# x of channel groups two to four turned by VectorE in 32 by 32 squares, from a new load layout, with SP's waits for it moved

## The chip, the cores and the metric

The kernel runs on one core of one Trainium2 chip. The metric is the device time of one execution in microseconds (us), as the median of several executions. One further execution was recorded by the profiler, and all rows below come from that one.

## The reference, cut to what matters

```python
# x (128, 32, 512), cond_128 (128, 128), fside_S_0 (32,) is the bias
out = lax.conv_general_dilated(x, weight, window_strides=(1,), padding=[(4, 4)],
        dimension_numbers=('NCH', 'OIH', 'NCH'), feature_group_count=4)      # 9 taps, 8 channels in and out per group
h = out + einsum('nd,od->no', c, c_weight)[:, :, None] + bias[None, :, None]
xt = h.reshape(-1, 512)                                                      # 4096 rows
y = (silu(xt @ W_gate.T) * (xt @ W_up.T)) @ W_down.T                         # 512 -> 1376 -> 512
return x + y.reshape(x.shape)
```

## The kernel before, in words

The 32 channels fall into four convolution groups of 8, and the whole kernel goes group by group (`g` = 0 to 3 in the code; "group one" in this text is `g` = 0). A group has 8 channels of 128 samples, so 1024 rows for the feed-forward part, kept as two halves of 512 tokens.

All products are made in fp32r with three terms (hi by hi, lo by hi, hi by lo): ScalarE rounds an operand to its `hi` part and VectorE subtracts it to get the `lo` part. For each of the 11 slices of 128 hidden features (`f`) a first phase makes seven products (`product(g, f, kind)`, kinds 0 to 6) of 6 matmuls each. One pass over such a slice is called an iteration here. ScalarE and VectorE make sigmoid, silu and the gated result from them. A second phase (`down`) multiplies the gated slices with W_down, in 22 units of 12 matmuls.

The convolution of group `g + 1` is woven into the iterations of group `g`. It runs in 8 steps `k` (`k = f - lag(g)`; lag is 1 for `g` = 0, and 0 otherwise). A step covers 64 positions. It needs x with (position, channel) on the partitions and the sample along the row:

- SP loads a chunk of 128 positions (two steps) of x into `x_in` (L344), 512 KB with one DMA. The sample is on the partitions.
- GpSimd copies half of it into `x_blk` with the channel innermost (`block_x`, L305).
- TensorE transposes `x_blk` in four 128 by 128 squares into the bank `xt_ps` (`turn_x`, L604), behind product 1 of the iteration.
- ScalarE makes `xt_hi` from the bank and VectorE `xt_lo` (`split_x`, L843 and L1070).
- TensorE multiplies with the Toeplitz operands made from `toep` (`conv_step`, L624 and L629), behind product 3 of the iteration, for step `k - 1`. The second three matmuls (L629) wait for the split of step `k` as well.
- VectorE adds the context and writes the result into `win` (`read_conv`, L1162). There is one `win` for a chunk, so the first `read_conv` of a chunk waits until the chunk before has left it.
- SP moves `win` into `stage` with one 64 KB DMA for each window of 16 positions (`stage_step`, L336, four DMAs a step). It does so for two steps at once, at the end of every second iteration.

TensorE, ScalarE, VectorE and GpSimd each have their order written out by hand. SP has one too: at each iteration of group one it loads W_gate and W_up for three slices later (`load_nat`), stores the seven split weights of the next slice to DRAM (`save_products`, L365), and in later groups it refills the ring of 16 slots from there (`refill`, L389, seven an iteration), each slot when the product that used it is done. At the end of the iteration come the load of x (after `x_blocked`) and the staging.

In group one the weights are also made: TensorE transposes the W_gate and W_up slices (`turn_gate`, `turn_up`), ScalarE and VectorE split them, and GpSimd mixes two of the seven (`mix_t`, `mix_t_lo`). `copy_chain` (L843) carries the sums from one product to the next through ScalarE.

## Time and profile before

| | us |
|---|---|
| median of 3 runs | 764.38 (764.04 to 764.9) |
| the profiled execution | 765.41 |
| its span, first to last instruction | 763.6 |
| mean granted TensorE clock | 0.999 |

The span is what the rows cover; 1.8 us of the profiled execution lie around it. Start times in rows are us from the start of the span. A matmul's record overlaps the next one's, so the pace of TensorE is read from the starts, not from the durations. For two or more merged instructions of a line (x2, x4) the time is that of the merged stretch.

### The profile page before, as it was taken

The numbers are of one execution on the slowest core, as the hardware profiler recorded it, in microseconds if no ns is written. First come the engines' busy times: TensorE is split into PE (matmuls) and PEld (weight loads), VectorE is DVE, ScalarE is ACT, GpSimd is POOL, SyncE is SP. The second block draws the span as 40 slices with busy tenths as digits, with TensorE's granted clock in tenths as the row PEclk, the third lists the DMA queues.
The fourth block names the chain that finished last, engine by engine and source line by source line (L and its number), as shares of the span: only waits on it lengthen the run. The fifth ranks groups of instructions, "written<-read, shape, count | busy, mean of one in ns | idle before, by whom it ended". The sixth has DMA issues, their size and how long they took to land.

```text
span 763.6 us, 10287 instructions
## 1 busy us (share of the span) xinstructions
PE 749.9 (98%) x3465; PEld 611.4 (80%) x3465; DVE 426.9 (56%) x703; ACT 275.3 (36%) x519; POOL 79.6 (10%) x111
## 2 busy tenths in 40 slices
PE   7989999999999999999999999999999999999998
PEld 6768888878888887887888878787788888887886
DVE  3897776764765555446735545445763444445224
ACT  4555555443433233324422332233431233333221
POOL 4334434110000111001000100100000000000000
PEclk9999999999999999999999999999999999999999
DMA  6486666679988578667435867667443876766412
GB/s 184 125 316 235 222 226 236 219 221 312 356 266 262 166 206 221 172 179 218 163 114 187 268 176 209 193 191 218 140 140 109 295 197 195 193 191 181 140 27 111
DMA packets 113684, 152.37 MB, mean 200 GB/s; under 512 B 11138, under 2 KB 49186, under 8 KB 113634
## 3 DMA queue, kind: packets, MB, share of 16 engines
q1 hardware_dynamic: 113152, 151.51, 63.7%
q8 instruction: 29, 0.48, 0.3%
q10 hardware_dynamic: 482, 0.21, 0.1%
q14 instruction: 21, 0.17, 0.1%
HBM read 108.95 MB, written 34.34 MB: 188 GB/s over the span
## 4 chain that ended last, share of the span: by engine, by line
PE 90%; issue 3%; SPq 2%; DMA 2%; DVE 1%; POOL 1%; ACT 0%; POOLq 0%; DVEq 0%
PE bank L711 51%; PE bank L774 31%; PE bank L624 2%; PE bank L629 2%; PE bank L604 2%; SPq L336 2%; DMA stage<-win 1%; PE bank L667 1%; PE bank L638 1%; PE bank L649 0%; DVE g_all L1277 0%; POOL g_all L526 0%; PE bank L586 0%; DVE win L1162 0%; POOL t_all L513 0%
## 5 line engine op out<-in xcount | busy, mean ns | idle before, releaser
L711 PE MATMUL bank<-hc_hi,ring 128*128 128x512 f32 (+1 forms) x1204 | 376.5, 394 | 5.0 <-DVE ring L1070 2.0
L711 PEld LDWEIGHTS bank<-hc_hi,ring 128*128 128x128 f32 (+1 forms) x1204 | 219.5, 185 | 54.6 <-issue 5.0
L711 PE MATMUL bank<-hc_lo,ring 128*128 128x512 f32 (+1 forms) x602 | 235.1, 391 | 0.0
L774 PE MATMUL bank<-ring,g_hi 128*128 128x512 f32 (+1 forms) x704 | 218.6, 392 | 0.0
L774 PEld LDWEIGHTS bank<-ring,g_hi 128*128 128x128 f32 (+1 forms) x704 | 131.2, 188 | 28.0 <-DVE g_lo L1070 0.8
L843 ACT ACTIVATE mix<-bank 128x512 f32<-128x512 f32 (+1 forms) x129 | 77.1, 598 | 208.5 <-PE bank L711 208.5
L774 PE MATMUL bank<-ring,g_lo 128*128 128x512 f32 (+1 forms) x352 | 137.1, 390 | 0.0
L711 PEld LDWEIGHTS bank<-hc_lo,ring 128*128 128x128 f32 (+1 forms) x602 | 111.5, 185 | 26.2
L1070 DVE TENSOR_TENSOR g_lo<-g_all,g_hi 128x512 fp32r<-128x512 f32 (+1 forms) x88 | 60.9, 695 | 83.7 <-ACT g_hi L843 83.7
L843 ACT ACTIVATE g_hi<-g_all 128x512 fp32r<-128x512 f32 (+1 forms) x88 | 55.1, 629 | 114.1 <-PE bank L774 114.0
L1243 DVE TENSOR_TENSOR mix<-bank,mix 128x512 f32<-128x512 f32 (+1 forms) x43 | 29.7, 691 | 87.2 <-ACT mix L960 87.0
L774 PEld LDWEIGHTS bank<-ring,g_lo 128*128 128x128 f32 (+1 forms) x352 | 66.1, 188 | 14.1
L305 POOL COPY x_blk<-x_in 128x512 f32<-128x512 f32 x24 | 28.0, 1166 | 325.5 <-DMA x_in<-in_x 166.4
L1238 DVE TENSOR_TENSOR mix<-bank,mix 128x512 f32<-128x512 f32 (+1 forms) x43 | 29.5, 687 | 37.5 <-ACT mix L843 37.5
L1233 DVE TENSOR_TENSOR mix<-mix 128x512 f32<-128x512 f32 (+1 forms) x43 | 29.7, 692 | 34.8 <-ACT mix L954 34.7
L960 ACT ACTIVATE mix<-bank 128x512 f32<-128x512 f32 (+1 forms) x43 | 25.7, 598 | 43.2 <-PE bank L711 43.2
L1228 DVE TENSOR_TENSOR mix<-bank,mix 128x512 f32<-128x512 f32 (+1 forms) x43 | 29.7, 691 | 11.2 <-PE bank L711 6.0
L843 ACT ACTIVATE xt_hi<-bank 128x512 fp32r<-128x512 f32 (+1 forms) x33 | 15.9, 510 | 55.1 <-PE bank L604 55.1
L1248 DVE TENSOR_TENSOR mix<-bank,mix 128x512 f32<-128x512 f32 (+1 forms) x43 | 29.7, 691 | 8.1 <-PE bank L711 6.8
L1162 DVE TENSOR_TENSOR win<-bank,ctxb 128x512 f32<-128x512 f32 (+1 forms) x24 | 16.1, 670 | 30.4 <-DMA stage<-win 21.5
L1070 DVE TENSOR_TENSOR hc_lo<-stage,hc_hi 128x512 fp32r<-128x512 f32 x50 | 32.6, 691 | 0.8 <-ACT hc_hi L843 0.7
L843 ACT ACTIVATE hc_hi<-stage 128x512 fp32r<-128x512 f32 x50 | 28.6, 618 | 2.9 <-DMA stage<-g_all 2.8
(141 smaller groups left out, 562.1 us busy)
## 6 DMA issues: line engine op xcount, KB each, us to landing
ring<-saved SPq DMA_DIRECT2D x319, 256.0 KB, 2.9
saved<-ring SPq DMA_DIRECT2D x99, 256.0 KB, 2.6
g_all<-in_x SPq DMA_DIRECT2D x32, 256.0 KB, 3.7
out_y<-g_all SPq DMA_DIRECT2D x32, 256.0 KB, 3.6
x_in<-in_x SPq DMA_DIRECT2D x13, 512.0 KB, 5.1
stage<-win SPq DMA_DIRECT2D x96, 64.0 KB, 2.8
w_nat<-in_L_ffn_W_gate SPq DMA_DIRECT2D x10, 256.0 KB, 3.9
w_nat<-in_L_ffn_W_up SPq DMA_DIRECT2D x10, 256.0 KB, 3.9
```

What stands on the lines that cost most here:

```text
L305: copy(blocks(grp, k)[:, :, :, :], x_place(grp, k // 2)[:, :, r0:r0 + WB * R] .rearrange("n c (b r) -> n b r c", r=R)).then_inc(x_blocked_ ...
L711: mm = pe.matmul(bank[0:w, :], wt, hv, start=fresh and q == 0 and t == 0, stop=q == 1 and t == 2, skip_group_check=not fresh)
L774: mm = pe.matmul(acc(half, tt)[:], gs, wd, start=f == 0 and t == 0, stop=f == FC - 1 and t == 2)
L843: return act.activation(dst, src, ACT.Copy)
L960: act.activation(act_b[0:w], chain_ps[f % 2][0:w, :], ACT.Sigmoid).then_inc(sig_b_done, 1)
L1070: return dve.tensor_tensor(dst, src, hi_part.bitcast(F32), ALU.subtract)
L1162: last = dve.tensor_tensor(to[:, w0:w0 + n, :], conv_bank(grp, k)[:, 0:n * P].rearrange("p (w n) -> p w n", w=n), ctxb[:, grp:grp + 1, :]. ...
L1228: dve.tensor_tensor(act_a[0:w], second_ps[0:w, :], copy0[0:w], ALU.add).then_inc(gate_a_done, 1)
L1233: dve.tensor_tensor(act_a[0:w], act_a[0:w], sig_a[0:w], ALU.mult).then_inc(silu_a_done, 1)
L1238: dve.tensor_tensor(copy4[0:w], third_ps[0:w, :], copy4[0:w], ALU.add).then_inc(up_b_done, 1)
L1243: dve.tensor_tensor(act_b[0:w], chain_ps[f % 2][0:w, :], act_b[0:w], ALU.mult).then_inc(silu_b_done, 1)
L1248: dve.tensor_tensor(copy2[0:w], third_ps[0:w, :], copy2[0:w], ALU.add).then_inc(up_a_done, 1)
```

## The change

For groups two to four x no longer goes through GpSimd and TensorE. SP loads each chunk with eight DMAs of 64 KB instead of one of 512 KB: partition `32 quad + n` of `x_in` gets, for both channels of the pair `quad`, the samples `n`, `n + 32`, `n + 64` and `n + 96`. VectorE turns half of such a chunk in one instruction, in squares of 32 by 32, into `x_blk` (now also seen as `x_turn`), with (channel, position) on the partitions. ScalarE and VectorE split that directly from there. VectorE does this at the head of the iteration, ahead of `gate_a`.

The partitions now have the channel outermost and the position in it innermost, so the rows of `toep` for groups two to four are put in that order once: GpSimd makes a permutation matrix `reorder`, TensorE multiplies `toep` with it in three matmuls of 192 columns (behind product 1 of the first iteration, where the first transposes of group two were), and ScalarE copies the results back ahead of its first Toeplitz split. The wait of TensorE for the last residual sums goes from `turn_x` to `conv_head`.

SP's work for the convolution goes to the head of its iteration. Each step is staged alone (four DMAs in every iteration for `k` = 2 to 9, instead of eight in every second one). The loads of chunks 1 to 3 come at `k` = 1, 3, 5 and wait for the turn of step `k`, where they came at the ends of `k` = 0, 2, 4 behind GpSimd's copy.

```diff
@@ -116,6 +116,7 @@
             x_gate = sb("x_gate", [P, KC, P], F32, early)
             t_all = sb("t_all", [P, 4, 2, P], F32, early)
             up1 = sb("up1", [P, TOK], F32R, early)
+            reorder = sb("reorder", [P, P], F32, early)
         g_hi = sb("g_hi", [P, NG, TOK], F32R)
         g_lo = sb("g_lo", [P, NG, TOK], F32R)
         stage = sb("stage", [P, KC, CG, P])
@@ -305,6 +306,15 @@
             copy(blocks(grp, k)[:, :, :, :], x_place(grp, k // 2)[:, :, r0:r0 + WB * R]
                  .rearrange("n c (b r) -> n b r c", r=R)).then_inc(x_blocked_first if grp == 0 and k == 0 else x_blocked, 1)
 
+
+
+        QUAD = 32
+        NB, CQ = P // QUAD, CG // (P // QUAD)
+        x_turn = x_blk[:, :, :, :].rearrange("n b r c -> n (b r c)")
+
+        def x_split_from(grp, k):
+            return xt_bank(grp, k)[:] if grp == 0 else x_turn
+
         def xt_at(grp, k):
             return (k if grp == 0 else k % 2) * WB * P
 
@@ -341,8 +351,15 @@
         @block.sync
         def _(sp):
             def load_x(grp, i):
+                if grp > 0:
+                    for quad in range(NB):
+                        for c in range(CQ):
+                            sp.dma_start(x_in[quad * QUAD:(quad + 1) * QUAD, c::CQ, :],
+                                         x[:, grp * CG + quad * CQ + c, i * P:(i + 1) * P].rearrange("(b n) l -> n b l", b=NB)
+                                         ).then_inc(x_loaded, LD)
+                    return
                 sp.dma_start(x_place(grp, i), x[:, grp * CG:(grp + 1) * CG, i * P:(i + 1) * P]
-                             ).then_inc(x_first_loaded[i] if grp == 0 else x_loaded, LD)
+                             ).then_inc(x_first_loaded[i], LD)
 
             def load_nat(f):
                 w = width(f)
@@ -429,6 +446,15 @@
                 if g > 0:
                     refill(product_at(g, 0, 0))
                 for f in range(FC):
+                    k = f - lag(g)
+                    if g + 1 < G and k == 2:
+                        for kind in range(KINDS):
+                            sp.wait_ge(hc_done[kind], hc_count(g, 1, kind))
+                    if g + 1 < G and 2 <= k < STEPS + 2:
+                        stage_step(g + 1, k - 2)
+                    if g + 1 < G and k in (1, 3, 5):
+                        sp.wait_ge(x_turned, STEPS * (g + 1) + k + 1)
+                        load_x(g + 1, (k + 1) // 2)
                     if g == 0 and f + 3 < FC:
                         load_nat(f + 3)
                     if g == 0 and f == FC - 2:
@@ -438,20 +464,10 @@
                         save_products(f + 1)
                     for fk in phase1[7 * f + 1:7 * f + 8]:
                         refill(product_at(g, *fk))
-                    k = f - lag(g)
-                    if g + 1 < G and k in (0, 2, 4):
-                        sp.wait_ge(x_blocked, STEPS * (g + 1) + k + 1)
-                        load_x(g + 1, k // 2 + 1)
-                    if g + 1 < G and k == 2:
-                        for kind in range(KINDS):
-                            sp.wait_ge(hc_done[kind], hc_count(g, 1, kind))
-                    if g + 1 < G and k in (2, 4, 6, 8):
-                        stage_step(g + 1, k - 2)
-                        stage_step(g + 1, k - 1)
                 if g == 0:
                     save_down(0)
                 if g + 2 < G:
-                    sp.wait_ge(x_blocked, STEPS * (g + 2) - 1)
+                    sp.wait_ge(x_turned, STEPS * (g + 2))
                     load_x(g + 2, 0)
                 for m, (f, half) in enumerate(units(g)):
                     if g == 0 and half == 0 and f + NDOWN < FC:
@@ -486,13 +502,8 @@
                                pattern=[[-1, TAPS], [-TAPS, CG]], channel_multiplier=1).then_inc(consts, 1)
 
             def block_x(grp, k):
-                if grp == 0:
-                    pool.wait_ge(x_first_loaded[k // 2], LD)
-                else:
-                    pool.wait_ge(x_loaded, LD * (KC * (grp - 1) + k // 2 + 1))
-                if grp > 0:
-                    pool.wait_ge(x_turned, STEPS * grp + k)
-                elif k > 1:
+                pool.wait_ge(x_first_loaded[k // 2], LD)
+                if k > 1:
                     pool.wait_ge(x_turned, k - 1)
                 copy_block(pool.tensor_copy, grp, k)
 
@@ -536,6 +547,8 @@
             block_x(0, 5)
             block_x(0, 6)
             block_x(0, 7)
+            pool.wait_ge(consts, 8)
+            pool.tensor_copy(reorder[:].rearrange("p (m r) -> p m r", r=R), ident[:].rearrange("p (r m) -> p m r", r=R)).then_inc(consts, 1)
             wrap(1)
             mix_t(0)
             mix_t_lo(0)
@@ -543,15 +556,11 @@
             mix_h_first(1)
             for g in range(G):
                 for f in range(FC):
-                    if g + 1 < G and f == 0:
-                        block_x(g + 1, 0)
                     if g == 0 and f + 2 < FC:
                         wrap(f + 2)
                     if g == 0 and f + 1 < FC:
                         mix_t(f + 1)
                         mix_t_lo(f + 1)
-                    if g + 1 < G and lag(g) <= f < STEPS - 1 + lag(g):
-                        block_x(g + 1, f + 1 - lag(g))
 
         @block.tensor
         def _(pe):
@@ -588,23 +597,32 @@
                 mm.then_inc(toep_mm, 1)
 
             def turn_x(grp, k):
-                if grp == 0 and k == 0:
+                if k == 0:
                     pe.wait_ge(x_blocked_first, 1)
-                else:
-                    pe.wait_ge(x_blocked, STEPS * grp + k)
-                if grp == 0 and k == 0:
                     pe.wait_ge(conv_w_ready, 1)
-                elif grp == 0 and k > 1:
+                else:
+                    pe.wait_ge(x_blocked, k)
+                if k > 1:
                     pe.wait_ge(xt_lo_done, k - 1)
-                elif grp > 0:
-                    pe.wait_ge(xt_lo_done, STEPS * grp + k)
-                if k == 0 and grp >= 2:
-                    pe.wait_ge(y_added, 2 * OB * (grp - 1))
                 for b in range(WB):
                     mm = pe.transpose(xt_bank(grp, k)[:, b * P:(b + 1) * P], blocks(grp, k)[:, b, :, :], ident[:])
                 mm.then_inc(x_turned, 1)
 
+            def reorder_toep():
+
+                pe.wait_ge(toep_done, 2)
+                pe.wait_ge(consts, 9)
+                pe.wait_ge(xt_lo_done, STEPS)
+                pe.wait_ge(g_done[1], 1)
+                for grp in range(1, G):
+                    to = conv_ps if grp == G - 1 else xt_ps
+                    at = (grp - 1) % 2 * QN * CG
+                    mm = pe.matmul(to[:, at:at + QN * CG], reorder[:], toep[:, grp, :, :], start=True, stop=True)
+                mm.then_inc(toep_mm, 1)
+
             def conv_head(grp):
+                if grp > 1:
+                    pe.wait_ge(y_added, 2 * OB * (grp - 1))
                 pe.wait_ge(t_lo_done, grp + 1)
                 pe.wait_ge(xt_lo_done, STEPS * grp + 1)
                 if grp == 1:
@@ -811,8 +829,8 @@
                         turn_up(2)
                     if conv and k == 1:
                         conv_head(g + 1)
-                    if conv and 0 <= k < STEPS:
-                        turn_x(g + 1, k)
+                    if g == 0 and k == 0:
+                        reorder_toep()
                     if g == 0 and f == FC - 1:
                         turn_down(0)
                     product(g, f, 2)
@@ -847,6 +865,11 @@
                     act.wait_ge(toep_done, 2)
                 else:
                     act.wait_ge(conv_done, CPG * grp)
+                if grp == 1:
+                    act.wait_ge(toep_mm, 2)
+                    hi(toep[:, 1:G - 1, :, :], xt_ps[:, 0:(G - 2) * QN * CG].rearrange("p (g q o) -> p g q o", g=G - 2, o=CG))
+                    hi(toep[:, G - 1, :, :], conv_ps[:, 0:QN * CG].rearrange("p (q o) -> p q o", o=CG)).then_inc(toep_done, 1)
+                    act.wait_ge(toep_done, 3)
                 hi(ta_hi[:], toep[:, grp:grp + 1, HALO:QN, :])
                 hi(tb_hi[:, TB0:P], toep[:, grp:grp + 1, 0:HALO, :]).then_inc(t_hi_done, 1)
 
@@ -855,9 +878,9 @@
                     act.wait_ge(conv_done, CPG * grp + (k if k >= 2 else 0))
                 act.wait_ge(x_turned, STEPS * grp + k + 1)
                 at = xt_at(grp, k)
-                last = hi(xt(grp)[0][:, at:at + WB * P], xt_bank(grp, k)[:])
+                last = hi(xt(grp)[0][:, at:at + WB * P], x_split_from(grp, k))
                 if grp > 0 and k % 2 == 0 and k > 0:
-                    last = hi(xt_hi[:, 2 * WB * P:], xt_bank(grp, k)[:, 0:P])
+                    last = hi(xt_hi[:, 2 * WB * P:], x_turn[:, 0:P])
                 last.then_inc(xt_hi_done, 1)
 
             def take_slot(s):
@@ -1107,12 +1130,21 @@
                     lo(t[0], toep[:, grp, HALO:QN, :], t[1])
                     lo(t[2][:, R - HALO:, :], toep[:, grp, 0:HALO, :], t[3][:, R - HALO:, :]).then_inc(t_lo_done, 1)
 
+            def turn_x(grp, k):
+                dve.wait_ge(x_loaded, LD * CG * (KC * (grp - 1) + k // 2 + 1))
+                if grp == 1 and k == 0:
+                    dve.wait_ge(x_turned, STEPS)
+                else:
+                    dve.wait_ge(xt_lo_done, STEPS * grp + k)
+                l0 = k % 2 * WB * R
+                dve.transpose(x_turn, x_in[:, :, l0:l0 + WB * R].rearrange("p m (w r) -> p w m r", r=R)).then_inc(x_turned, 1)
+
             def split_x(grp, k):
                 dve.wait_ge(xt_hi_done, STEPS * grp + k + 1)
                 at = xt_at(grp, k)
-                last = lo(xt(grp)[1][:, at:at + WB * P], xt_bank(grp, k)[:], xt(grp)[0][:, at:at + WB * P])
+                last = lo(xt(grp)[1][:, at:at + WB * P], x_split_from(grp, k), xt(grp)[0][:, at:at + WB * P])
                 if grp > 0 and k % 2 == 0 and k > 0:
-                    last = lo(xt_lo[:, 2 * WB * P:], xt_bank(grp, k)[:, 0:P], xt_hi[:, 2 * WB * P:])
+                    last = lo(xt_lo[:, 2 * WB * P:], x_turn[:, 0:P], xt_hi[:, 2 * WB * P:])
                 last.then_inc(xt_lo_done, 1)
 
             def w_lo(f, kind, src):
@@ -1318,6 +1350,8 @@
                     n, k = FC * g + f, f - lag(g)
                     more = g == 0 and f + 1 < FC
                     last = f == FC - 1
+                    if conv and 0 <= k < STEPS:
+                        turn_x(g + 1, k)
                     gate_a(n, f)
                     if conv and k == 1:
                         read_head(g + 1)
```

## Rows read from the trace of the kernel before

**Rows 1.** The page: busy time of each engine, and the granted TensorE clock in 40 slices.
```profile
PE 749.9 (98%) x3465; PEld 611.4 (80%) x3465; DVE 426.9 (56%) x703; ACT 275.3 (36%) x519; POOL 79.6 (10%) x111
...
PEclk9999999999999999999999999999999999999999
```

**Rows 2.** The chain that ended last: start, us, what (two pieces).
```profile
302.95 0.44 PE bank L604 x4
...
595.16 102.17 PE bank L711 x450
```

**Rows 3.** Windows, one iteration of group one, one of group two: length, busy times.
```profile
77.84:90.20 12.36, 12.36 (x62) 10.18 (x61) 8.78 (x17) 6.57 (x15) 4.56 (x7) 1.00 0.65 210
247.90:259.29 11.39, 11.39 (x53) 9.39 (x53) 6.18 (x11) 3.68 (x7) 2.23 (x2) 1.00 0.61 172
```

**Rows 4.** Timeline, first iteration (f = 1): start, us, engine, line, what [idle before <-releaser].
```profile
47.38 0.60 PE L604 MATMUL bank<-ident,x_blk 128*128 128x128 f32 x4
49.95 0.73 PE L711 MATMUL bank<-hc_hi,ring 128*128 128x512 f32 x2 [1.97 <-DVE ring L1070]
...
57.35 0.70 PE L711 MATMUL bank<-hc_hi,ring 128*128 128x512 f32 x2 [1.20 <-issue]
...
47.95 0.69 DVE L1221 TENSOR_TENSOR g_all<-bank,mix 128x512 f32<-128x512 f32 x1
48.56 1.33 DVE L1070 TENSOR_TENSOR ring<-t_all,ring 128x256 fp32r<-128x256 f32 x2
...
56.67 0.58 ACT L843 ACTIVATE mix<-bank 128x512 f32<-128x512 f32 x1
```

**Rows 5.** Timeline, setup: matmuls in plain f32 of 128 columns (two records each).
```profile
30.11 0.49 PE L576 MATMUL bank<-g_all 128*128 128x128 f32 x2
...
30.95 0.49 PE L576 MATMUL bank<-g_all 128*128 128x128 f32 x2
```

**Rows 6.** The page, groups of instructions: xcount | busy us, mean ns | idle before, releaser.
```profile
L305 POOL COPY x_blk<-x_in 128x512 f32<-128x512 f32 x24 | 28.0, 1166 | 325.5 <-DMA x_in<-in_x 166.4
...
L1228 DVE TENSOR_TENSOR mix<-bank,mix 128x512 f32<-128x512 f32 (+1 forms) x43 | 29.7, 691 | 11.2 <-PE bank L711 6.0
```

**Rows 7.** Timeline of PE and DVE, iterations f = 4 and 5 of group one.
```profile
85.62 0.62 PE L711 MATMUL bank<-hc_hi,ring 128*128 128x512 f32 x2
...
90.89 0.40 PE L629 MATMUL bank<-xt_hi,tb_hi 128*128 128x512 f32 x1
...
86.43 0.68 DVE L1261 TENSOR_TENSOR g_all<-mix 128x512 f32<-128x512 f32 x1
87.03 0.68 DVE L1257 TENSOR_TENSOR g_all<-mix 128x512 f32<-128x512 f32 x1
...
89.12 0.68 DVE L1070 TENSOR_TENSOR xt_lo<-bank,xt_hi 128x512 fp32r<-128x512 f32 x1
...
101.48 0.88 DVE L1070 TENSOR_TENSOR xt_lo<-bank,xt_hi 128x512 fp32r<-128x512 f32 x2
```

**Rows 8.** Timeline of DVE and PE, iteration f = 2 of group two.
```profile
257.44 0.89 DVE L1070 TENSOR_TENSOR xt_lo<-bank,xt_hi 128x512 fp32r<-128x512 f32 x2
...
259.82 0.40 PE L629 MATMUL bank<-xt_hi,tb_hi 128*128 128x512 f32 x1
```

**Rows 9.** Two lines of SP: ns to issue one DMA (min/median/max), us to landing.
```profile
L336 SPq DMA_DIRECT2D stage<-win x96: 552/598/1657, 85.0 to 522.0; - x96
...
DMA to landing us min/median/max: 2.4/2.6/4.5
...
L344 SPq DMA_DIRECT2D x_in<-in_x x13: 379/426/943, 1.2 to 472.2; - x13
```

**Rows 10.** Timeline of SP, end of iteration f = 4 of group two.
```profile
290.07 5.08 SPq L336 DMA_DIRECT2D stage<-win  x8
```

**Rows 11.** Who waited for whom: us in total, times, longest us.
```profile
DVE win L1162 <- DMA stage<-win: 21.5, 6, 4.4
...
PE bank L711 <- DVE mix L1238: 1.9, 3, 0.8
```

More of the change, by code:

```diff
@@ L590, in turn_x @@
             def turn_x(grp, k):
-                if grp == 0 and k == 0:
+                if k == 0:
                     pe.wait_ge(x_blocked_first, 1)
+                    pe.wait_ge(conv_w_ready, 1)
                 else:
-                    pe.wait_ge(x_blocked, STEPS * grp + k)
-                if grp == 0 and k == 0:
-                    pe.wait_ge(conv_w_ready, 1)
-                elif grp == 0 and k > 1:
+                    pe.wait_ge(x_blocked, k)
+                if k > 1:
                     pe.wait_ge(xt_lo_done, k - 1)
-                elif grp > 0:
-                    pe.wait_ge(xt_lo_done, STEPS * grp + k)
-                if k == 0 and grp >= 2:
-                    pe.wait_ge(y_added, 2 * OB * (grp - 1))
                 for b in range(WB):
```

## The prediction, made before the changed kernel was run

> **What bounds the kernel now.** I read the page first. TensorE is busy for 749.9 of 763.6 us at a granted clock that never leaves its upper level (2.4 GHz), VectorE for 56%, GpSimd for 10% [rows 1]. So the question is only what TensorE issues and where it waits. The chain that ended last gives its pace: 450 matmuls of 512 columns in 102.17 us, 0.227 us each, and four transposes of x take 0.44 us of it [rows 2]. The windows then show the two kinds of iteration. One of group one is 12.36 us long and one of group two 11.39, TensorE is busy in all of both, VectorE in 8.78 and 6.18 [rows 3]. Where x is turned, TensorE is therefore the bound, with other engines close only in group one. The waits say where it stands still after the first iteration: 1.9 us in three places, behind `up_b` (L1238), which stands on VectorE behind a `read_conv` that waited for the staging DMAs for up to 4.4 us [rows 11]. The timeline of the first iteration shows two more stops, of 1.97 and 1.20 us, where VectorE's and ScalarE's backlog from the setup sets the time [rows 4].
>
> **What is removed.** TensorE loses 24 blocks of four transposes (three groups, eight steps). Each is on the path, so 24 x 0.44 = 10.56 us go [rows 2]. One block is an exception: the first, at 47.38, stands ahead of the stop that ends at 49.95 [rows 4], so its 0.44 us was time in which TensorE would have waited anyway. That leaves 10.12. GpSimd's 24 copies (28.0 us, [rows 6]) were beside everything, so they are worth nothing by themselves.
>
> **What VectorE gets.** 24 turns of 128x512. The trace has no such operation. From below it is bounded by nothing I can defend except a small part of a normal instruction, so I take 0.30 us. From above by GpSimd's copy of the same half chunk in 16-element runs, 1.17 us. The nearest row is a VectorE pass over 128x512 f32, which lasts 0.69 us and costs 0.60 when another follows at once (86.43 to 87.03) [rows 6, 7]. I take 0.60, since the turn, too, reads and writes each element once.
>
> The Trainium skill (VectorE: DVE Perf Modes, The three transpose paths) gives 311 ns for a turn of 128x128 in bf16 on VectorE. As an estimate from that page, four such widths would be 1.24 us if time grew with width, and the sum would come out near the dear case below. No row here shows it.
>
> The turn stands ahead of `gate_a` and `split_x`, so each `xt_lo` ends 0.60 later against the end of the iteration before, while TensorE asks for it 0.44 earlier. It asks at the first L629. In group one, iteration f = 4, `xt_lo` ends at 89.80 and L629 starts at 90.89: margin 1.09, after the change 1.09 - 0.44 - 0.60 = 0.05. For even k it is 102.36 against 90.89 + 12.36 = 103.25: 0.89 - 1.04 = -0.15 [rows 3, 7]. Three such steps (k = 2, 4, 6) cost 0.45. In group two the margin at an even k is 259.82 - 258.33 = 1.49, so 0.45 stays [rows 8], and there the turn is free. Without that margin it would cost up to 0.60 in each of 16 iterations. What waits behind the turn on VectorE (`gate_a`, the weight splits, silu) is used by TensorE later than this.
>
> **The first iteration.** VectorE works without a gap from about 44 to 57 us there, and the stop that ends at 57.35 is for `copy_chain` of kind 4, which ScalarE ends at 57.25 behind `t_all` from VectorE [rows 4]. The first turn goes straight into this backlog: +0.60. The three matmuls of `reorder_toep` stand where the first transposes were, and wait for the first gated result of the second half, at 48.64. Plain f32 matmuls of 128 columns come in pairs 0.84 apart, 0.42 each [rows 5], so one of 192 columns is at most 0.63 and three 1.9. They end near 50.5 instead of 49.95; TensorE then reaches the second stop 0.6 later, at 56.75, and still has to wait until 57.95. So they cost nothing beyond the 0.60, and 1.9 if the stops were not there. ScalarE's two copies of `toep` out of the banks are each no longer than the 0.58 of a 128x512 one [rows 4], and `copied2` is ready about when TensorE asks for it, 2.7 us after 50.5. GpSimd's one copy into `reorder` lies in setup ahead of a wait for VectorE; it is at most a full 128x512 copy, 1.17.
>
> **What SP gets.** A load of a chunk becomes eight DMAs of 64 KB. The nearest row is the staging DMA of the same size: 0.60 to issue (at most 1.66) and 2.6 to land (at most 4.5); a whole chunk took 0.43 to issue [rows 9]. So a load is 4.8 us instead of 0.4, for 12 loads some 52 us more of SP. SP now also waits at the head of iterations k = 1, 3, 5, for a turn that ends at 87.63 + 0.60 = 88.23, which is 2.6 us after the iteration's start [rows 7]. Behind this wait stand the eight loads, then `load_nat`, `save_products` and the refills. The refills have 16 slots of six matmuls as lead, 16 x 1.36 = 21.8 us, against a delay of about 7.4 (2.6 + 4.8), and a landing of a few us. The saved weights and next slices of W are used more than an iteration later. So this is hidden. For x itself: issued at 7.4, landed by 10.0 to 11.9, and wanted by VectorE 11.39 - 0.44 + 2.0 = 12.95 after the same start. One to three us are left.
>
> The Trainium skill (DMA: Bandwidth & Descriptors, Measured) speaks against this edit: it advises batching to 1 MiB and calls transfers under 64 KB dominated by descriptors. In the trace eight pieces of 64 KB are issued in 5.08 us and overlap in flight [rows 9, 10], so the rule bears on SP's time and not on when x is there.
>
> **What the staging gives.** Before, SP issued two steps together in 5.08 us, from 290.07 on [rows 10], behind seven refills and the load of x; `read_conv` waited for the last. Now the first half has gone an iteration earlier and the second is first in SP's queue: issued by 2.4 after the head, landed by 5.0 to 6.9, about when `read_conv` wants to run. VectorE's six waits (21.5 us) should shrink to at most 1 or 2 us each, and TensorE's 1.9 us with them [rows 11]. I take 1.85 as gain; if it doesn't come, nothing.
>
> **Sum.** -10.12 + 0.60 + 0.45 - 1.85 = -10.92. Against the profiled execution that is 765.41 - 10.92 = 754.5. The median shown is 1.03 lower, so 753.5.
>
> **Rivals.**
> - *The turn is dear* (1.17). For: x is read in runs of 16, and GpSimd's copy was slow. Against: each element still passes once. The first iteration costs 0.57 more; group one's margins become -0.52 (four odd steps) and -0.72 (three even), 4.24 in place of 0.45; later even steps lose 0.12 six times. 753.5 + 0.57 + 3.79 + 0.7 = 758.5.
> - *Group one doesn't get shorter.* VectorE has 9.4 of 11.9 us to do there in a fixed order, and its chain through ScalarE may simply become the pace. Then its seven 0.44 are not gained: 753.5 + 3.1 - 0.45 = 756.1. Against: TensorE has no wait there now.
> - *The staging gain stays out*: 755.4.
> - *x comes too late, and the kernel is slower.* One mechanism: SP's issue of a piece. If it takes d us and lands in 2.6, VectorE stands at the head of the next iteration from 2.6 + 8d + 2.6 > 13.4 on, so d > 1.02, and all of TensorE's inputs behind it. Nine loads (k = 1, 3, 5 in three groups) are exposed. The whole gain is eaten at 1.2 us each, d = 1.17; at d = 1.3 nine times 2.2 us give 773. For: a DMA with four runs a partition may be slower than any shown, and the largest staging issue is 1.66. Against: the medians.
> - *The change does nothing for the time*, because TensorE's freed slots turn into waits everywhere: 764.4. Nothing in [rows 3] speaks for it, as TensorE never pauses there.
>
> By the figure of the Trainium skill above the dear case would be the likeliest; no row of VectorE shows it.
>
> **Chances.** My sum 0.68 (own range 752.4 to 754.6), the dear turn 0.10, group one at its old length 0.08, no staging gain 0.06, x too late 0.06, nothing 0.02. A measurement of this kernel tells 0.2% (1.5 us) from no change. Faster: 0.92, within: 0.02, slower: 0.06. The range: down to 751.5 (a turn of 0.30 takes 0.3 and the 0.45 off, and the chain of the first iteration may fall to GpSimd's lighter load), up to the dear turn, 758.5.
>
> **What would show it.** After the change: no L604 after the first 30 us, three f32 matmuls near 49 us; the iteration of group one at 11.9 to 12.1 us and of group two at 10.95; VectorE's turn at 0.6 to 0.7; each x piece issued in about 0.6 us; no wait of `win` for the stage DMAs of over 2 us; the stop near 58 us still there. The prediction is wrong if the turn takes over 1.2 us, if VectorE shows long waits for `x_in`, or if TensorE shows waits for `xt_lo` in most iterations.

## The result

| | us |
|---|---|
| before, median of 4 runs | 764.64 (764.04 to 767.55) |
| changed, median of 4 runs | 753.26 (751.9 to 754.21) |
| ratio | 0.9854, 95% interval 0.9834 to 0.9873 |
| span of the profiled execution, before and after | 763.6 and 750.7 |

The changed kernel is 11.4 us faster by the medians, and 12.9 by the two profiled executions. The forecast was 753.5, with a range of 751.5 to 758.5. (The median before is higher than in the table ahead of the prediction because a fourth run, of 767.55, has been added.)

The page after the change, busy times, against [rows 1]:

```profile
PE 738.9 (98%) x3375; PEld 602.0 (80%) x3375; DVE 437.6 (58%) x727; ACT 274.6 (37%) x521; POOL 51.4 (7%) x88
```

TensorE has 90 matmuls fewer (96 transposes gone, three f32 matmuls of two records each come) and 11.0 us less of busy time, and it is as full as before. VectorE got 10.7 us more. Three windows after the change, two iterations of group one (odd k, even k) and one of group two, against [rows 3]:

```profile
89.16:101.06 11.90, 11.90 (x57) 9.74 (x56) 9.21 (x18) 6.48 (x16) 3.55 (x6) 1.00 0.78 258
101.06:113.16 12.10, 12.10 (x58) 9.71 (x56) 9.42 (x19) 6.69 (x16) 3.49 (x6) 1.00 0.65 226
244.34:255.27 10.93, 10.93 (x49) 9.01 (x48) 6.26 (x10) 3.07 (x8) 0.00 (x0) 1.00 0.75 229
```

A block of four transposes was worth 0.46 us: 12.36 to 11.90, and 11.39 to 10.93. In group one every even k gives 0.2 of it back.

The turn on VectorE and the pieces of x on SP, one line each (ns min/median/max), against [rows 6, 9]:

```profile
L1140 DVE STREAM_TRANSPOSE x_blk<-x_in x24: 700/704/708, 49.2 to 484.5; 128x512 f32<-128x512 f32 x24
...
L357 SPq DMA_DIRECT2D x_in<-in_x x96: 311/432/1294, 35.8 to 467.8; - x96
...
DMA to landing us min/median/max: 1.8/2.1/5.3
```

The turn took 0.70 us, about as a plain VectorE pass over 128x512 f32 (0.69), and not the 1.24 us estimated from the Trainium skill's bf16 figure (VectorE: DVE Perf Modes, The three transpose paths); a piece took 0.43 us to issue and not 0.60.

Waits after the change, against [rows 11]:

```profile
DVE win L1194 <- PE bank L647: 8.6, 16, 0.9
...
PE bank L729 <- issue: 1.4, 1, 1.4
```

No `read_conv` waits for the staging any more. Of TensorE's five stops of over 0.3 us from the first iteration to the last convolution step, two in the first iteration and three behind `up_b`, the two of the first iteration are left. The second of them ends where it did (57.35 before, [rows 4]):

```profile
48.77 1.21 PE L620 MATMUL bank<-toep,reorder 128*128 128x192 f32 x6 [1.93 <-DVE g_all L1253]
...
57.34 0.70 PE L729 MATMUL bank<-hc_hi,ring 128*128 128x512 f32 x2 [1.42 <-issue]
```

The account, from the starts of the 24 convolution steps in both traces: the first step comes 0.40 us earlier, the eighth and last in group one's iterations 2.50, the first in those of group two 3.40, the last there 7.43, the first in those of group three 8.32, the last there 12.85, and the rest of the span is as long as before. Inside groups two and three, iterations without a stop went from 11.4 to 10.93. The four with a stop had been 11.63, 12.37, 12.47 and 12.02 long, that is 0.21, 0.95, 1.05 and 0.60 above 11.4, and are 10.93 too: the stops were worth 2.8 us with the slower matmuls behind them. 23 blocks at 0.46 are 10.6. With the 2.8, and less 0.6 for the even k, this is 12.8.

### The profile page after: what moved, and what is told of

The parts are those of the page before. It is cut to its first block, busy times and chain, and to the rows that moved or that the text cites. A ratio compares the mean times of both kernels' runs of the same rounds, so it can differ in the third digit from the quotient of the medians.

```text
span 750.7 us, 10175 instructions
## 1 busy us (share of the span) xinstructions
PE 738.9 (98%) x3375; PEld 602.0 (80%) x3375; DVE 437.6 (58%) x727; ACT 274.6 (37%) x521; POOL 51.4 (7%) x88
## 4 chain that ended last, share of the span: by engine, by line
PE 94%; DVE 2%; DMA 1%; SPq 1%; ACT 1%; issue 1%; DVEq 0%
PE bank L729 55%; PE bank L792 32%; PE bank L647 3%; PE bank L642 3%; DVE hc_lo L1093 1%; SPq L346 1%; PE bank L685 1%; DMA x_in<-in_x 1%; PE bank L656 1%; PE bank L608 0%; PE bank L667 0%; DMA stage<-g_all 0%; DVE g_all L1309 0%; DVE g_all L1194 0%; DVE ring L1093 0%
## 5 line engine op out<-in xcount | busy, mean ns | idle before, releaser
L983 ACT ACTIVATE mix<-bank 128x512 f32<-128x512 f32 (+1 forms) x43 | 25.7, 598 | 43.2 <-PE bank L729 43.2
L861 ACT ACTIVATE xt_hi<-x_blk 128x512 fp32r<-128x512 f32 (+1 forms) x33 | 16.9, 539 | 65.2 <-DVE x_blk L1140 65.2
L1289 DVE TENSOR_TENSOR g_all<-mix 128x512 f32<-128x512 f32 (+1 forms) x43 | 29.4, 685 | 0.0
L1293 DVE TENSOR_TENSOR g_all<-mix 128x512 f32<-128x512 f32 (+1 forms) x43 | 29.3, 682 | 0.0
```

Source lines behind the costliest of these rows:

```text
L861: return act.activation(dst, src, ACT.Copy)
L983: act.activation(act_b[0:w], chain_ps[f % 2][0:w, :], ACT.Sigmoid).then_inc(sig_b_done, 1)
L1289: dve.tensor_tensor(g_all[0:w, f, 0, :], copy2[0:w], act_a[0:w], ALU.mult).then_inc(g_done[0], 1)
L1293: dve.tensor_tensor(g_all[0:w, f, 1, :], copy4[0:w], act_b[0:w], ALU.mult).then_inc(g_done[1], 1)
```

## The experiments

### The staging alone, in the kernel before

```diff
                 for f in range(FC):
+                    k = f - lag(g)
+                    if g + 1 < G and k == 2: (waits for hc_done)
+                    if g + 1 < G and 2 <= k < STEPS + 2:
+                        stage_step(g + 1, k - 2)
...
-                    if g + 1 < G and k in (2, 4, 6, 8):
-                        stage_step(g + 1, k - 2)
-                        stage_step(g + 1, k - 1)
```

> The kernel before with one edit of the change alone: SP stages each step by itself at the head of its iteration, the loads of x stay where they were. Theory: TensorE's four stops behind the staging in groups two and three go (their iterations of 11.63, 12.37, 12.47 and 12.02 us become 11.4), so 2.8 us less, 761.8 against 764.6, and no iteration of group one changes. Rival (the whole gain is that of TensorE's freed slots and the staging gives nothing): 764.6.

Measured: 762.48 us (10 runs) against 764.75, ratio 0.9969 (0.9955 to 0.9983). All iterations of groups two and three are 11.39 to 11.42 long, and VectorE's wait is

```profile
DVE win L1161 <- DMA stage<-win: 8.2, 4, 2.6
```

So this edit of SP alone is worth 2.3 us by the medians (1.3 to 3.4 by the interval), and it needs nothing of the rest.

### The old staging, in the changed kernel

The same edit backwards in the changed kernel: staging in pairs, at the end of every second iteration, all else as changed.

> The changed kernel with SP's staging put back in pairs at the end of every second iteration; all else as changed. Theory: VectorE's long waits for the staging come back in groups two and three, 21 us in six places, and TensorE stops in four of them for 0.2 to 1.2 us, a little longer than before since its iteration is 0.46 shorter: 2.8 to 4 us more, 756 to 757.3 against 753.3. Rival (in the new kernel VectorE and SP have room enough, since the load of x is no longer ahead of the staging there): under 1 us more.

Measured: 753.08 us, ratio to before 0.9845 (0.9824 to 0.9866), no different from the changed kernel. VectorE did wait:

```profile
DVE win L1195 <- DMA stage<-win: 14.9, 6, 3.0
```

but no wait was over 3.0 us, and TensorE never stopped. The theory failed: pairs at the end of an iteration are not what stopped TensorE. What the two kernels with pairs differ in on SP is the load of x, which the changed kernel no longer has ahead of them.

### The load of x behind the staging, in the kernel before

```diff
-                    if g + 1 < G and k in (0, 2, 4): (wait, load_x)
                     if g + 1 < G and k == 2: ...
                     if g + 1 < G and k in (2, 4, 6, 8):
                         stage_step(g + 1, k - 2)
                         stage_step(g + 1, k - 1)
+                    if g + 1 < G and k in (0, 2, 4): (wait, load_x)
```

> The kernel before, with only the order at the end of SP's iteration turned round: the pairs of staging first, then the load of x, still one DMA of 512 KB. Theory now: what made TensorE stop was the load issued right ahead of the staging; its 512 KB stand in the DMA queue before the windows, and the last window lands 3.9 us after its issue instead of about 2. With the load behind, read_conv waits under 3 us and TensorE's four stops go: 2.5 us less, 762.2, as when the staging was moved to the head. Rival (the stops come from the pairs being issued late, at the end of the iteration): 764.7.

Measured: 762.64 us (10 runs), ratio 0.9974 (0.9965 to 0.9983). No iteration of groups two and three has a stop. The waits are those of the run before:

```profile
DVE win L1162 <- DMA stage<-win: 14.9, 6, 3.0
...
DMA to landing us min/median/max: 2.3/2.6/3.6
```

Against [rows 11] the longest wait is 1.4 us shorter, and against [rows 9] the longest landing is 3.6 and not 4.5. At the same place of group two (284 to 300 us) the median landing of the eight windows was, before,

```profile
stage<-win SPq DMA_DIRECT2D x8, 64.0 KB, 3.8
```

and with the load behind

```profile
stage<-win SPq DMA_DIRECT2D x8, 64.0 KB, 2.8
```

The six places with a pair of staging show the cause. In the kernel before, four of them stand behind a load of x, and the median landings there are 3.1, 3.8, 3.7 and 3.7 us; the two without a load have 2.8 and 2.5. With the load behind, all six have 2.5 to 2.8. From the end of the last window's issue to `read_conv` it was 1.85, 3.35, 3.26 and 2.78 us behind a load, and it is 1.8 to 1.9 in all other cases of both traces. So at three places the windows landed later behind the 512 KB; at the first only SP's own time for the load (0.94 there) came ahead of them.

How late `read_conv` may be can be read from the kernel before, too. Its six waits were 3.51, 4.25, 3.23, 4.38, 3.90 and 2.28 us, three of them here:

```profile
274.72 0.69 DVE L1162 TENSOR_TENSOR win<-bank,ctxb 128x512 f32<-128x512 f32 x1 [3.51 <-DMA stage<-win]
...
321.28 0.69 DVE L1162 TENSOR_TENSOR win<-bank,ctxb 128x512 f32<-128x512 f32 x1 [3.23 <-DMA stage<-win]
...
457.08 0.69 DVE L1162 TENSOR_TENSOR win<-bank,ctxb 128x512 f32<-128x512 f32 x1 [4.38 <-DMA stage<-win]
```

The iterations with 3.51, 4.25, 4.38 and 3.90 are the four long ones, by 0.21, 0.95, 1.05 and 0.60 us, which is each time the wait less 3.3; those with 3.23 and 2.28 are not longer. A wait of `read_conv` costs TensorE nothing up to 3.3 us in this kernel, and all of what is above. Either of the two edits of SP's order keeps every wait under that, so the second has no stop left to remove (the two together were not run in the kernel before).

### Eight pieces, in the kernel before

```diff
             def load_x(grp, i):
+                if grp > 0:
+                    for c in range(CG):
+                        sp.dma_start(x_in[:, c, :], x[:, grp * CG + c, i * P:(i + 1) * P]).then_inc(x_loaded, LD)
+                    return
```

GpSimd's wait for the load counts all eight pieces.

> The kernel before, with each load of x of groups two to four made as eight DMAs of 64 KB, one for each channel, into the old layout. Theory: SP spends some 0.43 us on each piece, 3 us more for a load; the loads stand ahead of the staging at the ends of k = 2 and 4 there, so read_conv waits some 3 us longer in those four places of groups two and three, and TensorE with it: 764.6 + 4 x 2.5 to 3 = 775. In group one nothing. Rival (pieces are free wherever they stand): 764.6.

Measured: 784.02 us, ratio 1.0241 (1.0216 to 1.0266): slower than the theory said, by 9 us. Four iterations took 15.71, 17.71, 15.87 and 15.66 us instead of 11.4, and two of group one 13.4 and 13.2. One of the stops, and the granted clock behind it (last but two column of the windows):

```profile
280.58 1.19 PE L715 MATMUL bank<-hc_hi,ring 128*128 128x512 f32 x2 [2.71 <-DVE mix L1242]
```

```profile
276.00:280.00 4.00, 1.88 (x9) 1.22 (x7) 0.85 (x2) 1.20 (x2) 0.00 (x0) 1.00 0.61 168
280.00:282.00 2.00, 1.42 (x4) 1.16 (x4) 1.03 (x2) 0.00 (x0) 0.00 (x0) 0.51 0.94 282
282.00:284.00 2.00, 2.00 (x7) 1.62 (x6) 0.48 (x1) 0.00 (x0) 0.00 (x0) 0.63 0.74 280
284.00:286.00 2.00, 2.00 (x12) 1.66 (x12) 1.87 (x4) 0.55 (x2) 0.51 (x1) 1.00 0.68 161
```

The stop itself is 2.71 us, and the iteration is 4.3 us longer, because TensorE was then granted 1.2 GHz for about 3 us. Behind the longest stop, of 3.28 us, the granted clock was 0.50 from 308 to 314 us, and that iteration is the 17.71. In group one the theory had seen no cost, and there were stops of 0.79 and 0.59. Eight pieces at the old place in SP's order are a loss of 19 us. (These pieces are one channel each over 128 partitions, and not the 32 partitions by four runs of the changed kernel; a piece of either kind is 64 KB.)

### TensorE's slots put back

```diff
+                    if conv and 0 <= k < STEPS and g + k > 0:
+                        ... (waits for the bank)
+                        for b in range(WB):
+                            pe.transpose(xt_ps[:, b * P:(b + 1) * P], ident[:], ident[:])
```

> The changed kernel with 23 blocks of four transposes of the identity matrix put back where the transposes of x were (all but the first block); their result is used by nobody. Theory: TensorE's slots alone are worth 23 x 0.46 = 10.6 us, less 0.6 since the three overshoots of xt_lo in group one vanish: 763.3. Rival (the freed slots gave less, and the gain is from GpSimd's and ScalarE's relief): under 5 us more.

Measured: 764.07 us (10 runs), 10.8 above the changed kernel. Iterations are 12.36, 11.39 and 11.42, those of the kernel before without its stops. From the first convolution step to the last it is 9.54 us longer than the changed kernel: 22 blocks lie between those steps, and 22 x 0.46 less 0.6 is 9.5. The rest lies ahead of the first step: one more block, and the first iteration, where the granted clock of this profiled execution fell for a few us (0.83 and 0.74 in the stretches 48 to 52 and 52 to 56). So the freed slots carry about 10 us, and the relief of GpSimd in the iterations after the first nothing.

### Each turn twice

```diff
+                dve.transpose(x_turn, x_in[...]).then_inc(turned_once, 1)
+                dve.wait_ge(turned_once, STEPS * (grp - 1) + k + 1)
                 dve.transpose(x_turn, x_in[...]).then_inc(x_turned, 1)
```

> The changed kernel with each turn made twice on VectorE, the second after the first by a semaphore, 0.7 us more at the head of 24 iterations. Theory: the turn is at the edge of its cover. The trace of the changed kernel has xt_lo ready 0.2 us ahead of its first user at even k in group two and 0.1 us late in group one, so most iterations with a turn get 0.3 to 0.7 us longer: 8 to 12 us more in all, 761 to 765. Rival (VectorE has 42% idle, a turn more is hidden): under 2 us more.

Measured: 766.7 us (10 runs), ratio to before 1.0021 (1.0005 to 1.0037): 13.4 above the changed kernel, a little over the theory's range, and the whole gain is gone. TensorE waits for it directly:

```profile
PE bank L648 <- DVE xt_lo L1094: 7.3, 13, 0.7
```

Iterations are 12.6 to 12.86 in group one and 11.13 to 11.71 in two and three. From the first convolution step to the last it is 12.25 us longer than the changed kernel: 0.7 for each turn of k = 1 to 7 in group one, and 0.2 to 0.4 for the odd and 0.8 for the even steps in groups two and three. The turns of k = 0 in groups two and three cost nothing, since VectorE waits there anyway. (The rest of the 13.4 lies ahead of the first step, where the first turn stands. There, too, the granted clock of the profiled execution fell, 0.78 and 0.79 in the stretches 56 to 60 and 60 to 64.) So 0.7 us on an engine that is idle for 42% of the span costs on average nearly 0.6 in each of 21 iterations: the idle time lies elsewhere in the iteration. In the changed kernel's iteration f = 2 of group two the margin is 0.21 us: `xt_lo` ends at 255.75 and L647 starts at 255.96.

```profile
253.20 0.71 DVE L1140 STREAM_TRANSPOSE x_blk<-x_in 128x512 f32<-128x512 f32 x1
254.86 0.89 DVE L1093 TENSOR_TENSOR xt_lo<-x_blk,xt_hi 128x512 fp32r<-128x512 f32 x2 [0.38 <-ACT xt_hi L861]
...
255.96 0.41 PE L647 MATMUL bank<-xt_hi,tb_hi 128*128 128x512 f32 x1
```

### Sixteen pieces

Each load of x cut once more, two blocks of samples a piece, 32 KB each.

> The changed kernel with each load of x cut once more, sixteen DMAs of 32 KB. Theory: a piece costs SP 0.43 us, so a load takes 7 us instead of 3.7; the last piece lands by 2.6 + 7 + 2.1 = 11.7 us after the head of the iteration, VectorE wants it at 12.9: no change, 753.3. Rival (SP is already at its limit): VectorE waits for x_in at even k, and the time rises by 5 us or more.

Measured: 755.98 us, ratio 0.9884 (0.9854 to 0.9914), 2.7 above the changed kernel: between the two. In groups two and three the theory held but for one iteration of 11.1. In group one, where SP has the weights to move as well, VectorE waited for x once, TensorE with it, and TensorE for the slices of W_down twice:

```profile
DVE x_blk L1141 <- DMA x_in<-in_x: 1.1, 1, 1.1
PE bank L686 <- DMA w_nat<-in_L_ffn_W_down: 0.7, 2, 0.4
```

```profile
128.21 0.47 PE L648 MATMUL bank<-xt_hi,tb_hi 128*128 128x512 f32 x1 [1.12 <-DVE xt_lo L1094]
```

The iteration with that stop was the longest of group one, 13.24 us, and the way from group one's last step to the first of group two was 1.1 us longer, of which 0.7 are the two waits for W_down. A load did not take SP 7 us but 8.4 to 8.8 in group one, against 3.7 to 3.9 in the changed kernel. So the rival with x too late has its mechanism right, and it starts near the 8.2 us for a load (8 x 1.02) that the prediction gave: the loads of 7.6 to 8.1 us in group two cost nothing. Of the time lost, 2.6 us lie between the first convolution step and the last.

### GpSimd's copies put back

A copy of 128x512 into a spare tile at each old place in group one.

> The changed kernel with GpSimd's eight copies of 128x512 put back at their old places of group one; they copy the context sums into a spare tile that nobody reads. Theory: in the first iteration the turn's 0.6 us was paid for by GpSimd being through with its mixing earlier, so that VectorE's two splits of t_all took 0.75 and not 1.33 us; with the copy back the stop of TensorE that ends at 57.34 ends 0.5 to 0.7 us later, and the time is 0.6 us more, 753.9; the iterations after it stay as they are. Rival (the compensation came from somewhere else): the stop ends at 57.3 as before.

Measured: 753.81 us, ratio 0.9849 (0.9819 to 0.9879), and the stop ended at 57.06. But the first copy had no x to wait for and ran long before its old place, so this run tells nothing about the first iteration. It does show that the other seven copies cost nothing. The next run has one copy, behind the wait:

```diff
+            pool.wait_ge(x_loaded, LD * CG)
             for g in range(G):
                 for f in range(FC):
+                    if g == 0 and f == 0:
+                        pool.tensor_copy(spare, ctxb in 16-element runs)
```

> The changed kernel with one copy of 128x512 on GpSimd ahead of the first mixing of the loop, and this time behind a wait for the first chunk of group two, as in the kernel before. Theory: in the kernel before, GpSimd waited for that chunk until 43.3 us and then copied, and VectorE's splits of 48.6 us ran beside its mixing (1.33 us for the two); without both, VectorE got 0.58 us back, which paid the first turn. With both back the two splits take 1.3 us again and the stop of TensorE near 57.3 ends 0.5 us later. Rival (it is not GpSimd): 0.75 us for the splits, the stop ends where it did.

Measured: a single run, 753.24 us, so there is no interval. The first iteration, against [rows 4]:

```profile
43.49 1.11 POOL L559 COPY spare<-ctxb 128x512 f32<-128x512 f32 x1 [14.46 <-DMA x_in<-in_x]
...
48.05 1.41 POOL L533 TENSOR_TENSOR ring<-t_all,ring 128x256 fp32r<-128x256 f32 x2
```

```profile
48.75 1.33 DVE L1101 TENSOR_TENSOR ring<-t_all,ring 128x256 fp32r<-128x256 f32 x2
```

```profile
58.13 0.70 PE L737 MATMUL bank<-hc_hi,ring 128*128 128x512 f32 x2 [1.78 <-issue]
```

In the changed kernel the same two splits of VectorE were

```profile
43.64 3.66 DVE L1093 TENSOR_TENSOR hc_lo<-g_all,hc_hi 128x512 fp32r<-128x512 f32 x4
...
48.54 0.75 DVE L1093 TENSOR_TENSOR ring<-t_all,ring 128x256 fp32r<-128x256 f32 x2
```

because GpSimd's mixing was over by 46.15. With the copy back they take 1.33 us and the stop ends 0.79 later. Of the 0.79 only 0.56 is the copy's: VectorE is 0.23 us behind already at 42.54, against 42.31 in the changed kernel, before the copy starts, and so its four `hc_lo` splits begin at 43.87 and not at 43.64. The Trainium skill (SBUF — State Buffer, SBUF: two separate sides) says that a VectorE instruction with two SBUF inputs and a GpSimd instruction that reads SBUF hold one pair of ports in turn; the two lengths agree with it.

A trace with the real copy shows that these 0.58 us need not be lost there. In the kernel before with the staging moved, x came earlier, GpSimd copied at 41.08, and its mixing fell on the four `hc_lo` splits:

```profile
43.20 4.10 DVE L1069 TENSOR_TENSOR hc_lo<-g_all,hc_hi 128x512 fp32r<-128x512 f32 x4
...
48.55 0.75 DVE L1069 TENSOR_TENSOR ring<-t_all,ring 128x256 fp32r<-128x256 f32 x2
```

So the sum counts. From the start of the `hc_lo` splits to the pass that follows the two splits, or the turn behind them, it was 5.94 us before; 6.02, 6.28 and 5.57 in the three other traces of that kernel with another order or size of loads; 5.57 in the changed kernel without the turn's 0.63; and 6.13 here without it. With the copy VectorE loses 0 to 0.7 us more to GpSimd in the first iteration than without it, depending on what the mixing falls on, and 0.37 in the pair compared.

### The turn in VectorE's gap

```diff
-                    if conv and 0 <= k < STEPS:
-                        turn_x(g + 1, k)
+                    if conv and k == 0:
+                        turn_x(g + 1, 0)
                     gate_a(n, f)
...
                     up_b(n, f)
+                    if conv and 0 <= k < STEPS - 1:
+                        turn_x(g + 1, k + 1)
```

> The changed kernel with the turns of steps 1 to 7 moved from the head of their iteration into the one before, between up_b and silu_b, where VectorE waits 1.9 us for ScalarE's sigmoid. Theory: the 0.2 us that each even k of group one lost come back (iterations of 12.1 become 11.9), nothing else moves: 0.6 us less, 752.7. Rival (a turn there meets x_in before it has landed, since SP loads it in the same iteration): TensorE waits at odd k, 1 to 3 us more in nine places.

Measured: 752.92 us, ratio to before 0.9841 (0.9812 to 0.9871). From the first convolution step to the last it is 431.52 us long and the changed kernel 432.37, and group one's iterations are 11.87 to 11.91. VectorE waited three times for x, 1.6 us in all, at no cost. By the medians 0.3 us is less than the runs can tell. Its profiled execution shows one reason why it isn't more. After the first stop in the first iteration the granted clock fell:

```profile
44.00:48.00 4.00, 3.37 (x19) 2.58 (x17) 4.00 (x6) 2.44 (x6) 2.68 (x3) 1.00 0.96 331
48.00:52.00 4.00, 2.69 (x8) 2.63 (x9) 3.96 (x9) 0.44 (x2) 0.37 (x2) 0.68 1.02 378
52.00:56.00 4.00, 4.00 (x17) 3.23 (x17) 3.21 (x8) 3.68 (x10) 0.00 (x0) 0.90 1.00 324
```

```profile
49.30 2.16 PE L620 MATMUL bank<-toep,reorder 128*128 128x192 f32 x6 [1.94 <-DVE g_all L1253]
```

The three reorder matmuls took 2.16 us there and 1.21 in the trace of the changed kernel.

### The gap, and the stop filled

```diff
                 pe.wait_ge(xt_lo_done, STEPS)
+                for b in range(4 * WB):
+                    pe.transpose(xt_ps[:, b % WB * P:(b % WB + 1) * P], ident[:], ident[:])
                 pe.wait_ge(g_done[1], 1)
```

> The kernel with the turn in VectorE's gap, and sixteen transposes of the identity ahead of the three reorder matmuls, where TensorE otherwise stands still for 1.9 us; nobody uses their result. Theory: in some executions (mean clock 0.998) the granted clock fell to 1.2 GHz for a few us right after this stop, which cost 1.5 to 2 us; with the stop filled the clock stays at 2.4 GHz in all, and the median is that of the undisturbed ones with the turn in the gap, about 751.8. Rival (the fall of the clock has nothing to do with the stop, or the transposes make TensorE late): 752.9 or more, and runs at 0.998 as before.

Measured: 752.09 us (751.8 to 753.03, 4 runs), ratio to before 0.9837 (0.9824 to 0.9851). The mean clock was 0.999 or 1.000 in all four; of the four runs of the changed kernel two were at 0.998, and these took 754.0 and 754.2 against 751.9 and 752.5. The five runs with the turn in the gap alone were at 0.997 to 0.999. It is the fastest kernel of the study by its median, but its interval overlaps that of the changed kernel, so it is not shown to be faster than that one, only than the kernel before. Four runs do not settle either that the stop was the cause of the fall.

## Why the prediction was right

**What bounds the kernel** held. TensorE was full before and is full after, and about 10 us came with its slots, as the run with idle transposes shows.

**The price of a block** was 0.44 in the sum and 0.46 in the windows, probably since the first matmuls behind a block are a little slower and the piece of the chain didn't hold that. Over 23 blocks that is 0.5 us.

**The first block as an exception** held: both stops of the first iteration are still there, and the first convolution step came 0.40 us earlier, one block's worth and not two.

**The first iteration** (+0.60) was wrong, the measured value is -0.01. VectorE's turn did go into its backlog, and cost 0.63. Two things that the sum left out hid it. GpSimd's copy, costed at nothing, had held back its mixing, and without the copy VectorE lost 0.37 us less to GpSimd. And VectorE's row of passes began 0.23 earlier in the trace after (43.64 against 43.87). That is scatter: over all traces, of either kernel, it begins between 43.2 and 45.0. So the term by itself was 0.26, and that the stop ended at the same time is chance.

**The turn's 0.60** held (0.70 long, it costs 0.62 to 0.63 ahead of another pass). The margins were less sound than they looked. For even k of group one a loss of 0.15 was forecast and 0.2 measured. For group two 0.45 was forecast and 0.21 measured, since `xt_lo` now waits for ScalarE's `xt_hi`, which starts only after the turn. It was enough, and the double turn shows how little more was there.

**SP's load**: 3.7 to 3.9 us instead of 4.8 (the first one 4.5), landed in time. This step held, and the sixteen pieces show the point from which it no longer does. One slip stands in the rival on x: it lets VectorE ask for x at 13.4, where the working above it has 12.95. With 12.95 its limit is 0.97 us for a piece and not 1.02.

**The staging** (-1.85) had the sign right, the size too small (2.8 by the trace, 2.3 and 1.8 by the medians of the two runs in the kernel before) and the reason half right. I took the stops' waiting time, and the slower matmuls behind each and the fourth, short stop of 0.21 were not in it. As the reason I named the place of the pairs, behind seven refills and the load of x. The runs show that the load ahead is enough of a cause: with the pairs at their old place behind the refills and the load put behind them, all stops are gone, as they are with the staging moved to the head.

The larger errors in size all go one way and add up: 0.6 too much cost in the first iteration, and some 1.0 and 0.5 too little gain in staging and slots. Only the even k go the other way, with 0.15 too little cost. Together this takes the forecast gain from 10.9 to 12.9, that of the profiled pair. So the mechanism was right, but that the median lies within 0.3 us of the forecast is in part luck. The forecast was counted down from the profiled execution of the kernel before (765.41) and then lowered by its distance to the median. The median of four runs before is 764.64, 0.8 under that execution, and the median after is 0.7 above its own profiled one. Two of the four runs after, at a mean clock of 0.998, took some 2 us more than the others; where in them the clock fell is not recorded. Why the medians before lie below the profiled execution no run shows, only that the staging is worth 2.3 and 1.8 us by medians and 2.8 by that trace.

Of the rivals, the dear turn is ruled out by its 0.70 us, group one at its old length by the windows. That x comes too late was not the case but near, and the case without a staging gain is ruled out by the trace.

## What to carry to other kernels

Work moved off a full engine is worth its slot there, but price it at the place where it lands: an engine with 42% idle had 0.2 us free at the point that mattered. A large load issued right ahead of small transfers that somebody waits for can cost them more than its issue (here 0.4 us of issue, and 1.0 to 1.5 us of landing at three places of four); order SP's work by who waits, and cut or place loads behind. And price the removed work of an idle engine too: by what stood behind it, and by whom it slowed.

## What was not expected of the hardware

- Each of the four stops of TensorE of 2.4 to 3.3 us in groups two and three of the run with eight pieces was followed by 1.2 GHz, for some 3 us behind three of them and for over 6 us behind the longest, so that a stop of 2.71 us made an iteration 4.3 us longer. In the first iteration the length of the stop did not decide it. Stops of 1.92 to 1.94 us were followed by a fall in the traces of the sixteen pieces, the idle transposes and the turn in the gap. The stops of 1.93 and 1.97 us in the changed kernel and the kernel before were not, and neither was one of 2.77 us in the run with eight pieces. What decides it stays open.
- A pass of VectorE in 32 by 32 squares over 128x512 f32, read in 16-element runs, took 0.70 us, the same as a plain one.
- Two splits of 128x256 on VectorE took 1.33 us beside GpSimd's mixing and 0.75 without.
- Four loads of 512 KB issued ahead of pairs of staging took 5.1 to 6.1 us to land, and 3.8 to 4.3 us when issued behind them.
